# Rounding the attention input's high part on ScalarE instead of GpSimd, in a fused attention and routed-FFN kernel

## The chip, the cores and the metric

The kernel runs on one core of one Trainium2 chip. The metric is the device time of one execution in microseconds, the median of three runs. Everything is one program: a layer-norm with modulation, an attention whose probabilities are formed per head, a second layer-norm, and a feed-forward block that is applied to the best 512 tokens of each batch.

## The reference, cut to what matters

```python
sa, ca, ga, sb, cb, gb = mod[:, 0], ..., mod[:, 5]        # from silu(c) @ wmod
h = _layernorm(x) * (1 + ca) + sa                         # x: 8 x 1024 x 512, float32
q, k, v = h @ Wq + bq, h @ Wk + bk, h @ Wv + bv           # each reshaped to (b, 16 heads, 32, t)
attn = softmax(einsum('bhdt,bhds->bhts', k, v) * temperature)
x = x + ga * einsum('bhdt,bhts->bhds', q, attn)
h = _layernorm(x) * (1 + cb) + sb
# router scores, best 512 of 1024 tokens, gelu FFN 512 -> 2048 -> 512, scattered back
x = x + gb * FFN(h)
```

The change concerns the first `h` alone: the modulated input of the projections.

## The kernel before, in words

The attention runs over 32 groups of 256 rows (8 batches of GB = 4 groups). A group holds four heads, whose scores are 32 units of 128 x 1024, taken as 16 pairs. PSUM has three slots for units (`SLOTS = 3`), one bank `pj` for projections and one `acc` for the output. Each engine has its own program with the order of its work written out by hand, and semaphores alone tie them together:

- TensorE (`body` from L756): for each pair p it makes the scores of unit (p, 0), the products of pair p - 4 with the queries, the scores of unit (p, 1), and a piece of the next group's key, value or query projection (L657, L669). Scores wait until ScalarE has freed the slot of three units earlier.
- VectorE (`body`, L1250): the negated row maximum of each unit (L1142), and between these the division of the queries by the row sums (`q_over_sums`, L1189 and L1194, once per two pairs), gating (L1171), statistics (L1176, L1062), the router's dot product (L1162). In the first group alone it also clamps the gates in four instructions (`clamp_gates`, L1151 to L1157) behind pairs 4 and 5.
- ScalarE (`body`, L963): the exponential of each unit (L916), which waits for its maximum, and evacuations of the projections: a key or value piece (L887) between the two exponentials of pairs 2, 5, 8 and 11, queries at 13 and 15. In the first group it also moves the late modulation out of `acc` before pair 3's exponentials (L972).
- GpSimd (`body`, L1589): elementwise work in eight portions. A portion begins behind a division on VectorE (`behind_qn(b, g, j)`, which waits for the division that VectorE issues at pair 2j).
- SyncE's queue (`body`, L541) issues loads, stores, the replication of keys and values (L488), and the DMA transposes.

The input of group n is prepared two groups ahead. GpSimd normalises it into `xhat` and multiplies by the scale in its last portion (`begin_x`, L1453 and L1498). In portion 0 of the group after, it adds the shift (`plus_shift`, L1503), then rounds to the 16-bit high part `x16[:, 0]` (`high_x`, L1510). In portion 1 it makes the low part (`low_x`, L1515). SyncE waits for `s_hi` and issues four transposes of the high part, waits for `s_ht` and issues four of the low part (`transpose_x`, L480), and then goes on to wait for the residual and to load the next x (`load_x`, L441). In the first group it stores the clamped gates before all this (`store_modulation`, L509), behind `s_modv`, which the last clamp raises. The rounding occurs 30 times, in all groups but the last two.

Of the kernel before, what the change touches and what calls it, by code (L numbers as in the profile page):

```python
# [17 lines left out]
GB = T // TG  # L18
# [11 lines left out]
ALU = mybir.AluOpType  # L30
ACT = mybir.ActivationFunctionType
# [100 lines left out]
def block_phases(nc, x, w_qkv, b_qkv, temperature, w_router, w_ffn, c, w_mod, out, h_rows, mod_rows, first_rows, sel_rows, score_rows, r):  # L132
# [16 lines left out]
    with ExitStack() as ctx:  # L149
# [6 lines left out]
        def sem(name):  # L156
            return ctx.enter_context(nc.semaphore(name))
# [24 lines left out]
        xhat = room3[:, 0, 0:2, :]  # L182
# [9 lines left out]
        x16 = room2[:, S_LEN + 2 * KV_LEN:S_LEN + 3 * KV_LEN].rearrange("p (a s n) -> p a s n", a=2, s=SUBS)  # L192
# [129 lines left out]
        s_xm = sem("s_xm")  # L322
        s_xt = sem("s_xt")
# [8 lines left out]
        s_hi = sem("s_hi")  # L332
# [41 lines left out]
        def ring_at(p, h2):  # L374

            return 2 * p + h2
# [5 lines left out]
        def unit_no(b, g, u):  # L382

            return b * (GB * UNITS) + (g * UNITS + u + 1)

        def pair_no(b, g, p):

            return b * (GB * PAIRS) + (g * PAIRS + p + 1)

        def slot(b, g, v):  # L390

            return sc[:, ((b * GB + g) * RING + v) % SLOTS, :]

        def prepared(n):


            return 16 * 4 * SUBS * (n - 1)
# [235 lines left out]
        def stk_count(b, g):  # L633

            return b * (128 * GB // 2) + 128 * (g // 2 + 1)
# [237 lines left out]
        def _(act):  # L873
# [8 lines left out]
            def evac_kv(g, kk, count, free, src=pj[:]):  # L882

                act.wait_ge(kv_pe, count)
                if free is not None:
                    act.wait_ge(kv_split, free)
                nc.scalar.activation(kv32[kk % 2][:], src, ACT.Identity,  # L887
                                     scale=tempw_col[:, g:g + 1] if kk < 2 else 1.0 / WS).then_inc(kv_evac, 1)

            def evac_t(src, count, parts=False):  # L890

                act.wait_ge(t_pe, count)
                for cc in range(CC):
                    a = nc.scalar.activation(hT32[:, cc, :].rearrange("q (t s e) -> q s t e", t=2, s=SUBS),
                                             src[:, cc * 2 * P:(cc + 1) * 2 * P].rearrange("q (s t e) -> q s t e", t=2, s=SUBS),
                                             ACT.Identity, bias=mod_now[:, CC + cc:CC + cc + 1], scale=mod_now[:, cc:cc + 1])
                    if parts:
                        a.then_inc(t_part, 1)
                return a
# [10 lines left out]
            def exp_unit(b, g, p, h2):  # L910

                u = 2 * p + h2
                act.wait_ge(max_done, unit_no(b, g, u))
                if h2 == 0:
                    act.wait_ge(pv_done, pair_no(b, g, p))
                nc.scalar.activation(probs[:, u % PROBS, :], slot(b, g, ring_at(p, h2)), ACT.Exp,  # L916
                                     bias=nmax[:, u % PROBS:u % PROBS + 1],
                                     accum_out=rsum[:, (u // 4) % 2, u % 4:u % 4 + 1]).then_inc(slot_free, 1)

            act.wait_ge(s_now, 1)  # L920
            evac_t(sc[:, 2, :], 1, parts=True)
            act.wait_ge(s_bk, 2 * 16)
# [35 lines left out]
            def kept_high(n, cc, src):  # L958

                act.wait_ge(ft_pe, nth(n, CC, cc + 1))  # L960
                nc.scalar.activation(fT16[n % 2][0][:, cc, :], src, ACT.Identity).then_inc(ft_hi, 1)

            def body(b, last):  # L963
                for g in range(GB):
                    n4 = b * (GB * 4) + 4 * (g + 1)
                    n2 = b * (GB * 2) + 2 * (g + 1)
                    end = last and g == GB - 1
                    for p in range(PAIRS):
                        if b == 0 and g == 0 and p == LAG - 1:
                            act.wait_ge(pv_done, LAG)  # L970
                            act.wait_ge(s_one, 2)
                            nc.scalar.activation(mod_b, late_ps, ACT.Identity, bias=one_row[:, 0:1]).then_inc(s_modc, 1)  # L972
                        exp_unit(b, g, p, 0)
                        if p < 12 and p % 3 == 2 and not end:
                            evac_kv((g + 1) % GB, p // 3, n4 + p // 3 + 1, n4 + p // 3 - 1)
                        if (p == 13 or p == 15) and not end:
                            evac_q((g + 1) % 2, (p - 13) // 2, n2 + (p - 13) // 2 + 1)
                        if last and g == 1 and p == 2:
                            act.wait_ge(s_dot, 2 * (NG - 3) + 1)
                            nc.scalar.activation(r.e_neg[:, 0:LAST * TB], scores[:, AHEAD:AHEAD + LAST * TB], ACT.Exp, scale=-1.0).then_inc(s_exps, 1)  # L980
                        if end and p == 3:
                            for k in range(2):
                                for s in range(SUBS):
                                    act.wait_ge(s_stk[k][1][s], stk_count(LAST, GB - 1))
                            high_part(0)
                        if end and p == 11:
                            high_part(1)
                        if end and p - 1 in KEPT_AT:
                            kept_high(0, KEPT_AT.index(p - 1), aux[0])
                        exp_unit(b, g, p, 1)  # L990

            for b in range(B - 1):
                body(b, False)
# [420 lines left out]
        def _(pool):  # L1414
# [9 lines left out]
            for j in range(P // DH):  # L1424
# [4 lines left out]
                last = nc.gpsimd.affine_select(out=part, in_=part, compare_op=ALU.is_gt, fill=0.0, base=2 * DH * h2 + t,  # L1429
                                               pattern=[[-1, 2], [-2 * DH, 2], [-2, DH]], channel_multiplier=2)  # L1430
# [72 lines left out]
                nc.gpsimd.tensor_tensor(xhat, xhat, mod_x[:, 0:1, :].broadcast_to([P, SUBS, D]), ALU.add).then_inc(s_xm, 1)  # L1503
                pool.wait_ge(s_xm, 2 * (n - 1))

            def high_x(n):

                if n > 2:
                    pool.wait_ge(s_xt, prepared(n - 1))
                nc.gpsimd.tensor_scalar(x16[:, 0], xhat, 1.0, 1.0, ALU.mult, ALU.mult).then_inc(s_hi, 1)  # L1510

            def low_x(n):

                pool.wait_ge(s_hi, n + 1)
                nc.gpsimd.tensor_tensor(x16[:, 1], xhat, x16[:, 0], ALU.subtract).then_inc(s_ht, 1)  # L1515

            def begin_x(n):
# [71 lines left out]
            def body(b, last):  # L1589
                for g in range(GB):  # L1590
                    n4 = b * (GB * 4) + 4 * (g + 1)
                    n = b * GB + g + 2
                    nxt = (g + 1) % GB
                    prep = not (last and g >= GB - 2)
                    end = last and g == GB - 1

                    if b == 0 and g == 1:
                        pool.wait_ge(s_modst, 4 * 16)
                    behind_qn(b, g, 0)
                    if prep:  # L1600
                        plus_shift(n)
                        high_x(n)
                    if last and g == GB - 2:
                        store_kept(nc, r, sel_rows, range(2, 4))
                    if end:
                        gather_h(0, h_rows[0:T])
                    behind_qn(b, g, 1)
                    if prep:
                        low_x(n)
                    if not end:  # L1610
                        split_kv(nxt, 0, n4 + 1, n4 + 1 - 3)
                    if last and g == GB - 2:
                        store_kept(nc, r, sel_rows, range(4, 6))
                    behind_qn(b, g, 2)
                    residual(b, g)
                    if last and g == GB - 2:
                        store_kept(nc, r, sel_rows, range(6, TB))
                    if end:
                        break
                    behind_qn(b, g, 3)  # L1620
                    split_kv(nxt, 1, n4 + 2, n4 + 2 - 3)
                    normed_before(b, g)
                    behind_qn(b, g, 4)
                    h_times(b, g)
                    split_kv(nxt, 2, n4 + 3, n4 + 3 - 3)
                    behind_qn(b, g, 5)
                    h_plus(b, g)
                    split_kv(nxt, 3, n4 + 4, n4 + 4 - 3)
                    behind_qn(b, g, 6)
                    base_times(b, g)  # L1630
                    base_plus(b, g)
                    behind_qn(b, g, 7)
                    if n + 1 < NG:
                        begin_x(n + 1)
                    if last and g == GB - 3:
                        wait_alone(r.s_slot, 1)
                        store_kept(nc, r, sel_rows, range(0, 2))
# [76 lines left out]
```

## Time and profile before

| | |
|---|---|
| median of 3 runs | 2283.25 us (2282.88 to 2284.57) |
| the profiled execution's own time | 2283.22 us |
| its span, first to last instruction | 2281.5 us |
| TensorE busy | 2212.2 us (97%) |
| VectorE busy | 1890.5 us (83%) |
| ScalarE busy | 1431.7 us (63%) |
| GpSimd busy | 1398.7 us (61%) |
| mean granted TensorE clock | 0.993 of full speed |

The span is 1.7 us shorter than the execution's own time; that rest lies around the instructions. Busy shares are averages over two stages: the attention (to about 1,600 us), where VectorE is at nine tenths or more in every slice, and the feed-forward stage behind it, where VectorE falls to three to seven tenths.

### The profile page before, as it was taken

To read this page: it belongs to the slowest core of one execution; us is meant where nothing else is said; L and a number is where in the kernel's file an instruction comes from. 1 tells how busy PE (TensorE), PEld (TensorE's weight loads), DVE (VectorE), ACT (ScalarE), POOL (GpSimd) and SP (SyncE) were. 2 spreads that over 40 slices of the span, in tenths; PEclk is the share of its full clock that TensorE was granted. 3 is DMA by queue.
4 is the path that set the end of the run, shared out by engine and by line. 5 is a ranking of instruction groups with operands and counts; after the bars stand their busy time and mean duration, and the time that the engine had idled before them with its cause. 6 is when DMAs were issued, how large, how long until landed. Compare 5 with 4: busy or idle time off the path is not lost.

```text
span 2281.5 us, 35224 instructions
## 1 busy us (share of the span) xinstructions
PE 2212.2 (97%) x12410; PEld 840.0 (37%) x12410; DVE 1890.5 (83%) x2887; ACT 1431.7 (63%) x2478; POOL 1398.7 (61%) x1174
## 2 busy tenths in 40 slices
PE   6899999999999999999999999997899999999998
PEld 2233333333333333333333333331344444444443
DVE  6899999999999999999999999999873664563533
ACT  3688887888888888888888888888221111111110
POOL 6677887777888778887788877871642212302300
PEclk9999999999999999999999999999999999999999
DMA  7343344343335434444433533443432122112210
GB/s 255 79 104 88 92 108 96 95 103 95 91 90 122 84 93 114 85 101 100 98 89 89 127 82 91 97 84 94 139 88 70 41 66 70 61 47 70 68 31 19
DMA packets 218864, 206.06 MB, mean 90 GB/s; under 512 B 139256, under 2 KB 139288, under 8 KB 218176
## 3 DMA queue, kind: packets, MB, share of 16 engines
q1 hardware_dynamic: 208176, 174.12, 32.4%
q0 software_dynamic: 9728, 25.23, 3.5%
q10 hardware_dynamic: 784, 4.47, 0.5%
q8 instruction: 97, 1.59, 0.3%
q14 instruction: 79, 0.65, 0.1%
HBM read 71.37 MB, written 43.19 MB: 50 GB/s over the span
## 4 chain that ended last, share of the span: by engine, by line
PE 54%; DVE 32%; POOL 4%; issue 3%; SPq 3%; ACT 3%; DMA 1%; POOLq 0%; DVEq 0%; ACTq 0%
DVE nmax L1142 22%; PE sc L848 14%; PE sc L835 14%; PE sc L645 9%; PE acc L694 9%; PE pj L669 6%; POOL x L1530 3%; PE pj L657 3%; ACT probs L916 2%; DVE qn L1194 2%; DVE stats L1176 2%; DVE dot_out L1162 2%; SPq L480 1%; SPq L488 1%; DVE x L1171 1%
## 5 line engine op out<-in xcount | busy, mean ns | idle before, releaser
L916 ACT ACTIVATE probs<-sc,nmax 128x1024 f32<-128x1024 f32 x1024 | 1139.3, 1116 | 238.7 <-DVE nmax L1142 228.7
L1142 DVE TENSOR_REDUCE nmax<-sc 128x1 f32<-128x1024 f32 x1024 | 1206.1, 1212 | 28.3 <-PE sc L645 25.6
L694 PE MATMUL acc<-probs,qn 128*32 128x512 f32 x4096 | 546.6, 606 | 5.0 <-DVE x L1171 2.8
L1018 ACT ACTIVATE probs<-sc,b_col 128x512 f32<-128x512 f32 x128 | 87.9, 687 | 532.6 <-PE sc L835 519.1
L657 PE MATMUL pj<-room 128*128 128x512 f16 x1500 | 387.5, 381 | 2.7 <-POOL room L1483 2.7
L848 PE MATMUL sc<-room,probs 128*128 128x512 f16 x1536 | 355.5, 382 | 7.0 <-DVE probs L1362 4.1
L645 PE MATMUL sc<-room 128*128 128x512 f16 x1024 | 309.1, 384 | 23.1 <-ACT probs L916 13.7
L645 PE MATMUL sc<-stacks 128*128 128x512 f16 x1024 | 308.3, 383 | 11.7 <-ACT probs L916 10.2
L1360 DVE CAST probs<-probs 128x512 f16<-128x512 f32 x128 | 60.4, 472 | 292.1 <-ACT probs L1018 291.9
L848 PEld LDWEIGHTS sc<-room,probs 128*128 128x128 f16 x1536 | 150.8, 98 | 191.3 <-DVE probs L1362 5.0
L657 PEld LDWEIGHTS pj<-room 128*128 128x128 f16 x1500 | 144.2, 98 | 187.7 <-ACT room L887 12.2
L916 ACT ACTIVATION_READ_ACCUMULATOR probs<-sc,nmax 128x1 f32 x1024 | 202.8, 198 | 0.0
L669 PE MATMUL pj<-room 128*128 128x256 f16 x1512 | 185.6, 273 | 0.7 <-DVE room L1127 0.4
L645 PEld LDWEIGHTS sc<-room 128*128 128x128 f16 x1024 | 76.7, 98 | 294.1 <-ACT probs L916 196.0
L645 PEld LDWEIGHTS sc<-stacks 128*128 128x128 f16 x1024 | 75.9, 97 | 283.8 <-ACT probs L916 195.7
L835 PE MATMUL sc<-stacks,room 128*128 128x512 f16 x768 | 176.2, 379 | 0.0
L669 PEld LDWEIGHTS pj<-room 128*128 128x128 f16 x1512 | 147.0, 98 | 46.8 <-ACT qT L906 4.8
L694 PEld LDWEIGHTS acc<-probs,qn 128*32 128x32 f32 x4096 | 81.1, 108 | 224.0 <-issue 213.1
L1539 POOL TENSOR_TENSOR hbuf<-hbuf,rows 128x1024 f32<-128x1024 f32 x66 | 156.0, 2364 | 12.2 <-DVE qn L1194 8.9
L835 PE MATMUL sc<-qT,room 128*128 128x512 f16 x512 | 162.4, 379 | 0.0
L1472 POOL TENSOR_TENSOR room<-room 128x512 f16<-128x512 f32 x125 | 146.3, 1170 | 10.4
L1468 POOL TENSOR_TENSOR room<-room,k_bias 128x512 f32<-128x512 f32 x63 | 82.2, 1305 | 114.1 <-DVE qn L1194 109.1
(168 smaller groups left out, 2238.6 us busy)
## 6 DMA issues: line engine op xcount, KB each, us to landing
stacks<-room SPq DMA_DIRECT2D x512, 64.0 KB, 2.0
room<-room SPq DMA_DIRECT2D x508, 64.0 KB, 2.0
h_rows<-hbuf SPq DMA_DIRECT2D x132, 128.0 KB, 2.3
out<-base SPq DMA_DIRECT2D x132, 128.0 KB, 2.4
room<-in_L_attn_x SPq DMA_DIRECT2D x96, 128.0 KB, 2.6
rows<-mod_rows SPq DMA_DIRECT2D x32, 256.0 KB, 4.2
room<-in_L_ffn_W SPq DMA_DIRECT2D x8, 1024.0 KB, 5.3
probs<-in_L_wmod ACTq DMA_DIRECT2D x4, 1024.0 KB, 12.0
```

The costliest lines, as they stand in the source:

```text
L645: mm = nc.tensor.matmul(slot(b, g, v)[:, half * D:(half + 1) * D], stacks[g % 2][:, 0, hq, i * P:(i + 1) * P], stacks[g % 2][:, 1, hq, hal ...
L657: mm = nc.tensor.matmul(dst, hT16[par][:, a, cc, p * P:(p + 1) * P], w[:, z, cc, :], start=(t == 0), stop=(t == len(terms) - 1))
L669: mm = nc.tensor.matmul(dst[:, ci * 2 * P:(ci + 1) * 2 * P], wq16[:, z, cc, co * P:(co + 1) * P], hT16[par][:, a, cc, :], start=(t == 0), ...
L694: mm = nc.tensor.matmul(acc[at:at + DH, :], qn[:, (p // 2) % 2, p % 2, h2, :], probs[:, (2 * p + h2) % PROBS, half * D:(half + 1) * D], st ...
L835: mm = nc.tensor.matmul(ff[f % 2], w1_16[:, z, cc, f * P:(f + 1) * P], fT16[n % 2][a][:, cc, :], start=(t == 0), stop=(t == len(terms) - 1))
L848: mm = nc.tensor.matmul(ff2[kt], g16[:, nth(n, FC, f) % 3, a, kt * P:(kt + 1) * P], w2_16[:, z, f, :], start=(f == 0 and t == 0), stop=(f ...
L916: nc.scalar.activation(probs[:, u % PROBS, :], slot(b, g, ring_at(p, h2)), ACT.Exp, bias=nmax[:, u % PROBS:u % PROBS + 1], accum_out=rsum[ ...
L1018: nc.scalar.activation(g32[:, f % 2, :], ff[f % 2], ACT.Gelu_apprx_tanh, bias=b1_col[:, f:f + 1], scale=1.0 / WS).then_inc(gelu_done, 1)
L1142: nc.vector.tensor_reduce(nmax[:, u % PROBS:u % PROBS + 1], slot(b, g, ring_at(p, h2)), AX.X, ALU.max, negate=True).then_inc(max_done, 1)
L1468: nc.gpsimd.tensor_tensor(kv32[kk % 2][:], kv32[kk % 2][:], row, ALU.add).then_inc(kv_bias, 1)
L1472: nc.gpsimd.tensor_tensor(dst[:, 1], kv32[kk % 2][:], dst[:, 0], ALU.subtract).then_inc(kv_split, 1)
L1539: nc.gpsimd.tensor_tensor(dst, a, rows[:, row:row + 1, :].broadcast_to([P, SUBS, D]), op).then_inc(s_hm, 1)
```

## The change

ScalarE gets a function `high_x(n)`, called behind the second exponential of pair 1 in each of the 30 groups, and GpSimd loses its own. ScalarE's waits for the shift (`s_xm`), for the previous rounding (`s_hi`) and for the transposes that still read `x16` (`s_xt`). GpSimd's `low_x` now waits for ScalarE's rounding and for the same transposes.

```diff
@@ ScalarE
+            def high_x(n):
+                act.wait_ge(s_xm, 2 * (n - 1))
+                act.wait_ge(s_hi, n)
+                if n > 2:
+                    act.wait_ge(s_xt, prepared(n - 1))
+                nc.scalar.activation(x16[:, 0], xhat, ACT.Identity).then_inc(s_hi, 1)
...
                         exp_unit(b, g, p, 1)
+                        if p == 1 and not (last and g >= GB - 2):
+                            high_x(b * GB + g + 2)
@@ GpSimd
-            def high_x(n):
-
-                if n > 2:
-                    pool.wait_ge(s_xt, prepared(n - 1))
-                nc.gpsimd.tensor_scalar(x16[:, 0], xhat, 1.0, 1.0, ALU.mult, ALU.mult).then_inc(s_hi, 1)
...
             def low_x(n):
 
                 pool.wait_ge(s_hi, n + 1)
+                if n > 2:
+                    pool.wait_ge(s_xt, prepared(n - 1))
                 nc.gpsimd.tensor_tensor(x16[:, 1], xhat, x16[:, 0], ALU.subtract).then_inc(s_ht, 1)
...
                         plus_shift(n)
-                        high_x(n)
```

## Rows read from the trace of the kernel before

**Rows 1.** The page, part 4: the chain that ended last, shares by line.

```profile
DVE nmax L1142 22%; PE sc L848 14%; PE sc L835 14%; PE sc L645 9%; PE acc L694 9%; PE pj L669 6%; POOL x L1530 3%; PE pj L657 3%; ACT probs L916 2%; DVE qn L1194 2%; DVE stats L1176 2%; DVE dot_out L1162 2%; SPq L480 1%; SPq L488 1%; DVE x L1171 1%
```

**Rows 2.** Windows, one group: stretch, length, busy of PE, PEld, DVE, ACT, POOL, clock, DMA.

```profile
737.62:785.40 47.78, 47.54 (x293) 16.55 (x290) 46.66 (x65) 40.64 (x73) 38.21 (x32) 1.00 0.47 94
```

**Rows 3.** Timeline, GpSimd and VectorE, same group: start, length, instruction, idle before.

```profile
737.62 2.35 POOL L1503 TENSOR_TENSOR room<-room,f_lo 128x1024 f32<-128x1024 f32 x1 [0.32 <-DVE qn L1194]
740.06 1.36 POOL L1510 TENSOR_SCALAR room<-room 128x1024 f16<-128x1024 f32 x1
743.46 2.13 POOL L1515 TENSOR_TENSOR room<-room 128x1024 f16<-128x1024 f32 x1 [2.03 <-DVE qn L1194]
...
739.64 0.88 DVE L1162 SCALAR_TENSOR_TENSOR dot_out<-hbuf,router_row 128x512 bf16<-128x512 f32 x1
```

**Rows 4.** Timeline, ScalarE from the end of pair 1 to pair 3.

```profile
740.77 0.19 ACT L916 ACTIVATION_READ_ACCUMULATOR probs<-sc,nmax 128x1 f32 x1
741.70 1.11 ACT L916 ACTIVATE probs<-sc,nmax 128x1024 f32<-128x1024 f32 x1 [0.74 <-DVE nmax L1142]
742.80 0.68 ACT L887 ACTIVATE room<-pj,tempw_col 128x512 f32<-128x512 f32 x1
743.37 1.11 ACT L916 ACTIVATE probs<-sc,nmax 128x1024 f32<-128x1024 f32 x1
...
746.17 1.11 ACT L916 ACTIVATE probs<-sc,nmax 128x1024 f32<-128x1024 f32 x1 [0.50 <-DVE nmax L1142]
```

**Rows 5.** Groups by form, ScalarE rounding float32 to float16: busy us, mean ns.

```profile
L956 ACT ACTIVATE room<-room 128x2048 f16<-128x2048 f32 x8 | 15.3, 1907 | 13.7 <-DMA room<-in_L_ffn_W 13.7
```

**Rows 6.** Timelines of weight loads, matmuls and VectorE about pairs 3 and 4.

```profile
743.53 0.72 PEld L657 LDWEIGHTS pj<-room 128*128 128x128 f16 x4
...
746.16 0.60 PE L645 MATMUL sc<-room 128*128 128x512 f16 x2
...
744.92 3.47 DVE L1142 TENSOR_REDUCE nmax<-sc 128x1 f32<-128x1024 f32 x3
```

**Rows 7.** Timeline, GpSimd in the first group.

```profile
58.30 2.36 POOL L1503 TENSOR_TENSOR room<-room,f_lo 128x1024 f32<-128x1024 f32 x1 [0.21 <-DVE qn L1194]
...
67.66 2.35 POOL L1530 TENSOR_TENSOR x<-x,xt 128x1024 f32<-128x1024 f32 x1
```

**Rows 8.** Timeline, ScalarE in the first group.

```profile
56.18 1.11 ACT L916 ACTIVATE probs<-sc,nmax 128x1024 f32<-128x1024 f32 x1 [0.85 <-DVE nmax L1142]
...
58.94 0.69 ACT L972 ACTIVATE base<-acc,one_row 128x512 f32<-128x512 f32 x1
```

**Rows 9.** Timeline, VectorE in the first group.

```profile
59.67 0.69 DVE L1171 TENSOR_TENSOR x<-acc,rows 128x512 f32<-128x512 f32 x1 [0.29 <-ACT base L972]
...
63.67 0.63 DVE L1151 TENSOR_SCALAR hbuf<-base 64x512 f32<-64x512 f32 x1
64.23 1.75 DVE L1152 SCALAR_TENSOR_TENSOR hbuf<-base 64x512 f32<-64x512 f32 x1
...
66.10 0.50 DVE L1194 TENSOR_TENSOR qn<-qT,rinv 128x128 f32<-128x128 f32 x1
...
68.79 1.51 DVE L1155 TENSOR_SCALAR hbuf<-hbuf 64x512 f32<-64x512 f32 x1
```

**Rows 10.** Timelines of SyncE's queue and of VectorE, later in the first group.

```profile
71.04 1.31 SPq L509 DMA_DIRECT2D mod_rows<-base  x4
...
73.99 10.66 SPq L480 DMA_TRANSPOSE room<-room  x8
...
89.08 0.69 DVE L1062 BATCH_NORM_STATS2 stats<-xt 128x6 f32<-128x512 f32 x1 [6.63 <-DMA xt<-in_L_attn_x]
```

**Rows 11.** Windows in the first group, columns as in rows 2.

```profile
85.00:92.00 7.00, 0.95 (x8) 0.04 (x7) 2.92 (x4) 1.07 (x2) 1.60 (x2) 0.91 0.54 142
92.00:98.00 6.00, 5.81 (x18) 1.45 (x19) 4.49 (x7) 4.39 (x10) 4.36 (x4) 0.54 0.40 91
```

**Rows 12.** Source line L1162, all instances: duration ns, minimum/median/maximum.

```profile
L1162 DVE SCALAR_TENSOR_TENSOR dot_out<-hbuf,router_row x67: 679/852/1162, 54.0 to 1674.6; 128x512 bf16<-128x512 f32 x67
```

More of the change, by code:

```diff
@@ L1504, in plus_shift, with low_x @@
                 pool.wait_ge(s_xm, 2 * (n - 1))
-            def high_x(n):
+            def low_x(n):
+                pool.wait_ge(s_hi, n + 1)
                 if n > 2:
                     pool.wait_ge(s_xt, prepared(n - 1))
-                nc.gpsimd.tensor_scalar(x16[:, 0], xhat, 1.0, 1.0, ALU.mult, ALU.mult).then_inc(s_hi, 1)
-            def low_x(n):
-                pool.wait_ge(s_hi, n + 1)
                 nc.gpsimd.tensor_tensor(x16[:, 1], xhat, x16[:, 0], ALU.subtract).then_inc(s_ht, 1)
```

## The prediction

> **What bounds the kernel now.** I read the page's chain first. VectorE's row maximum holds 22% of it, far more than any other line of the attention [rows 1]. The windows then show how near the bound each engine is inside one group: of 47.78 us VectorE is busy 46.66 and ScalarE 40.64 [rows 2]. The reader is to see that VectorE has about 1.1 us to spare in a group, ScalarE 7.1 us, and TensorE (47.54 us, with modelled ends) little. GpSimd, the engine that is relieved, is busy 38.21 us and bounds nothing in this stretch. So what the change is worth is read from whether VectorE's order of work moves. I then went through the timelines at the place of the edit, first in an ordinary group, then in the first group, which stands differently.
>
> **Ordinary groups (29 of the 30).** Removed from GpSimd: one rounding of 1.36 us, at 740.06. Its next instruction, the low part, does not start when the rounding ends (741.42) but at 743.46, behind VectorE's division [rows 3]. So the removal starts nothing earlier on GpSimd; its idle time before the low part grows from 2.03 to about 3.4 us. Price: nothing, hidden by the wait for the division.
>
> Added to ScalarE: one rounding of 128 x 1024. The trace has none of this shape. From below, half of the 128 x 2048 rounding is 0.95 us [rows 5]; from above, the 128 x 1024 exponential is 1.11 us [rows 4]. I take 1.05, as the fixed part of an instruction is not halved. What it waits for is there: the shift ends at 737.62 + 2.35 = 739.97 [rows 3], and the read-out of pair 1's second exponential ends at 740.77 + 0.19 = 740.96 [rows 4]. Neighbouring instructions on ScalarE overlap by about a tenth (the evacuation ends at 743.48, the next exponential starts at 743.37 [rows 4]). So the rounding runs from 740.87 to 741.92, and the next exponential can start at 741.81 in place of 741.70. The 0.74 us for which ScalarE waited there [rows 4] takes nearly all of it; 0.11 us is left. In other groups this idle time differs by a tenth or so, and I allow 0.1 to 0.25.
>
> Who waits for that lag? Queued behind the rounding are the exponential of unit (2, 0), the evacuation of a key piece, and the next exponentials. The evacuation ends at 743.48 and TensorE loads weights for the next piece at 743.53 [rows 6], so TensorE can come up to 0.1 us late there. It passes that on to the scores of unit (4, 1), which now end at 746.16 + 0.60 = 746.76. The reduction that reads them is the third of the three from 744.92, each about 1.13 us apart, so it starts at 747.18 [rows 6]: 0.42 us to spare. ScalarE has 0.50 us idle before the exponential at 746.17 [rows 4], and its lag ends there. VectorE sees nothing: price 0 per group. If that cover were gone, it would be 0.11 to 0.25 us times 29, which is 3.2 to 7.3 us. From below, no gain either, except by rival four.
>
> SyncE is moved too: the four transposes of the high part start about 0.5 us later (741.92 for 741.42). Eight take 10.66 us in the queue [rows 10]. What stands behind them, the residual's wait and the loads of x, moves by the same half microsecond; it is needed at pair 9, seven pairs of 3 us later. GpSimd's added wait on the old transposes is one that it already had. Price 0.
>
> **The first group.** Here GpSimd is late. Its shift starts at 58.30 and ends at 60.66 [rows 7], while ScalarE starts unit (2, 0) at 56.18 after 0.85 us of idling [rows 8]. With the edit ScalarE stands at the rounding until 60.66, rounds for 1.05 us, and starts unit (2, 0) at about 61.67. That is 5.5 us later. Everything queued behind it moves by as much, among it L972, which takes the late modulation out of `acc` at 58.94 [rows 8] and would do so at 64.4. VectorE's gating at 59.67 waited for exactly this, by 0.29 us [rows 9], and moves to 65.2. From there VectorE runs without a gap through three maxima, two clamps, the division, two maxima and the other clamps. At its end SyncE starts storing the gates at 71.04 [rows 10].
>
> Some of the 5.5 us comes back, because VectorE's instructions in this stretch are now slowed by GpSimd, which will have become idle by then (it waits for the division of pair 4). L1152 takes 1.75 us [rows 9]. Its twin L1157 fits between the end of L1155 (68.79 + 1.51 = 70.30 [rows 9]) and 71.04 [rows 10], so it takes 0.7; 1.05 come back. L1151 (0.63) and the division (0.50) [rows 9] are slowed in the same way by an estimated half: 0.5 together. L1155 then starts 3.95 us later, at 72.74. It now ends 0.29 us after the residual on GpSimd does (67.66 + 2.35 = 70.01 [rows 7]), so it waited for that. The residual starts behind the division, which will be at 66.10 + 5.5 - 1.35 = 70.25 to 70.55, plus 0.15 for the signal: 70.7 to 73.05. L1155 then ends at 73.3 in place of 70.3. **3.0 us are left** of 5.5. The ends of this term are 2.5 (a little more comes back) and 5.5 (nothing does).
>
> These 3.0 us are on the path. The queue runs from 71.04 without a real pause: gates, eight transposes from 73.99, then the load of x, and VectorE stands idle 6.63 us for that load until 89.08 [rows 10]. All later groups hang on VectorE.
>
> **Sum.** 29 x 0 + 3.0 on the profiled execution's own 2283.22 us (span 2281.5 and 1.7 around it) is 2286.2. That execution lies 0.03 under the median, so I forecast 2286.3 us. A measurement of this kernel can tell about 0.2%, that is 4.6 us, from no change; the forecast is slower, by less than that.
>
> **Rivals.**
>
> *One: the stall arrives whole, and TensorE's clock falls.* Scores of unit (3, 1) need the slot that the late exponential frees, so TensorE stands still some 5 us before 62.9. After the quiet stretch from 85 to 92 (0.95 us busy in 7) the granted clock was 0.54 from 92 to 98, which is the 1.2 GHz level [rows 11]. At that level the products and scores ahead of the pair 4 maximum (about 1.6 us at full clock) cost about 1 us more than VectorE's work hides. With no give-back: 5.5 + 1.0 = 6.5, so 2289.8 us. For it: the stand-still is real. Against it: the pause here is shorter, and the slowed rows are plain. By the Trainium skill ("TensorE: Matmul & The Clock Gate", section "What's actually happening") an idle TensorE goes back to 1.2 GHz; the trace agrees for the longer pause (0.54), and no row shows one of 5 us.
>
> *Two: the lag of ordinary groups passes.* 3.0 + 3.2 to 7.3 gives 2289.5 to 2293.6 us. It decides from a lag of 0.42 us at unit (4, 1) in the group shown. The 0.1 us margins of other groups speak for it, the 0.50 us idle against.
>
> *Three, the other side: the first group's wait swallows the stall.* VectorE idles 6.63 us at 82.45 to 89.08 anyway, more than 5.5. If the load of x did not hang on the clamps, the delay would vanish there: 2283.3 us, no change. It decides as long as the stall stays under 6.63 us and the load keeps its time. Against it: the queue is in order, and the store of the gates starts with the last clamp's end [rows 10].
>
> *Four: VectorE is freed of contention.* The router's dot product takes 0.88 us beside GpSimd [rows 3] and 0.68 at its fastest [rows 12]. If the rounding were what slows it, 0.2 x 29 = 5.8 us would come back: 2283.3 + 3.0 - 5.8 = 2280.5 us. Against it: the dot product starts at 739.64, the shift ends at 739.97, and 739.97 + 0.55 is where it ends; the rounding starts only at 740.06 [rows 3], when the dot product is already under way. The Trainium skill says ("GPSIMD Engine Reference", section "1. Specifications") that the two engines share their SBUF interfaces, VectorE instructions with two SBUF inputs among those that contend. By that rule the removal should bring the 5.8 us; the trace agrees that there is contention (0.88 against 0.68) but puts it on the shift, which stays.
>
> **How the numbers follow.** Chances: forecast 0.55, rival one 0.17, two 0.10, three 0.12, four 0.06. The forecast's own range is 2285.7 to 2288.0. Leaving out rival four, the lower edge of three and the upper half of two, the range for 8 in 10 is 2283.0 to 2290.5 us. Slower by over 0.2% (over 2287.8): rivals one and two and a small part of the forecast, 0.31. Faster by over 0.2%: most of rival four, 0.05. Within: 0.64.
>
> **What the changed profile would show.** ScalarE: 30 roundings of 1.05 us, one of them in the first group behind some 5.3 us of idling for the shift, the others behind none. The exponential behind it 0.1 to 0.25 us late in ordinary groups, the length of a group unchanged (47.8 us for the one shown). GpSimd idle 3.4 us before the low part. VectorE's gating in the first group near 65.2, L1152 near 0.7 us, the gates stored near 74.0, the statistics of x near 92.1. I would be wrong if ordinary groups change their length, if ScalarE waits for the shift in them, or if the store of the gates is late by less than 2.5 or more than 5.5 us.

## The result, and the profile after

| | before | changed |
|---|---|---|
| median of 9 runs | 2283.25 us (2281.28 to 2285.91) | 2290.69 us (2289.64 to 2291.60) |
| span of the profiled execution | 2281.5 us | 2288.8 us |

The ratio is 1.003, with a 95% interval of 1.002 to 1.004: slower by 7.4 us, where 3.0 were forecast. The measured median lies 0.2 us beyond the upper end of the stated range (2290.5).

The ordinary groups first. The timelines of ScalarE, GpSimd and VectorE in the changed kernel, in the same group that [rows 3, 4, 6] show of before:

```profile
747.06 0.19 ACT L916 ACTIVATION_READ_ACCUMULATOR probs<-sc,nmax 128x1 f32 x1
747.15 1.04 ACT L926 ACTIVATE room<-room 128x1024 f16<-128x1024 f32 x1
748.10 1.10 ACT L916 ACTIVATE probs<-sc,nmax 128x1024 f32<-128x1024 f32 x1
...
752.49 1.11 ACT L916 ACTIVATE probs<-sc,nmax 128x1024 f32<-128x1024 f32 x1 [0.43 <-DVE nmax L1152]
```

```profile
743.92 2.37 POOL L1513 TENSOR_TENSOR room<-room,f_lo 128x1024 f32<-128x1024 f32 x1 [0.32 <-DVE qn L1204]
749.82 2.14 POOL L1521 TENSOR_TENSOR room<-room 128x1024 f16<-128x1024 f32 x1 [3.54 <-DVE qn L1204]
...
754.09 1.16 POOL L1482 TENSOR_TENSOR room<-room 128x512 f16<-128x512 f32 x1
```

```profile
749.30 0.29 DVE L1204 TENSOR_TENSOR qn<-qT,rinv 128x128 f32<-128x128 f32 x1
...
754.84 0.57 DVE L1204 TENSOR_TENSOR qn<-qT,rinv 128x128 f32<-128x128 f32 x1
```

The rounding takes 1.04 us and waits for nothing; the exponential behind it starts about 0.1 us after it could have, and ScalarE idles again (0.43 us) two units on. But GpSimd's low part starts at 749.82, which is 0.23 us behind the end of VectorE's division (749.30 + 0.29). In the kernel before it started at 743.46 [rows 3] against a division that ended at 743.27 (the first row below), 0.19 us. In the unrounded times of all 29 ordinary groups this distance is 0.18 us before; in the changed kernel it is 0.23 to 0.24, but for one group with 0.54. GpSimd's three instructions of the key split then all end later. VectorE's division of pair 4 ends 0.16 us behind the last of them in both kernels (755.41 against 755.25, and 749.04 against 748.88), and takes 0.57 us where it took 0.52. The rows of before:

```profile
742.98 0.29 DVE L1194 TENSOR_TENSOR qn<-qT,rinv 128x128 f32<-128x128 f32 x1
...
748.52 0.52 DVE L1194 TENSOR_TENSOR qn<-qT,rinv 128x128 f32<-128x128 f32 x1
```

```profile
747.72 1.16 POOL L1472 TENSOR_TENSOR room<-room 128x512 f16<-128x512 f32 x1
```

The first group, against [rows 7 to 10]. ScalarE and VectorE of the changed kernel:

```profile
59.62 1.06 ACT L926 ACTIVATE room<-room 128x1024 f16<-128x1024 f32 x1 [5.13 <-POOL room L1513]
60.59 1.10 ACT L916 ACTIVATE probs<-sc,nmax 128x1024 f32<-128x1024 f32 x1
...
63.33 0.69 ACT L980 ACTIVATE base<-acc,one_row 128x512 f32<-128x512 f32 x1
```

```profile
64.06 0.69 DVE L1181 TENSOR_TENSOR x<-acc,rows 128x512 f32<-128x512 f32 x1 [5.73 <-ACT base L980]
...
67.86 1.23 DVE L1152 TENSOR_REDUCE nmax<-sc 128x1 f32<-128x1024 f32 x1 [0.85 <-PE sc L645]
69.00 0.41 DVE L1161 TENSOR_SCALAR hbuf<-base 64x512 f32<-64x512 f32 x1
69.34 0.68 DVE L1162 SCALAR_TENSOR_TENSOR hbuf<-base 64x512 f32<-64x512 f32 x1
...
70.14 0.29 DVE L1204 TENSOR_TENSOR qn<-qT,rinv 128x128 f32<-128x128 f32 x1
...
72.61 0.64 DVE L1165 TENSOR_SCALAR hbuf<-hbuf 64x512 f32<-64x512 f32 x1
...
92.12 0.69 DVE L1072 BATCH_NORM_STATS2 stats<-xt 128x6 f32<-128x512 f32 x1 [6.70 <-DMA xt<-in_L_attn_x]
```

ScalarE stands 5.13 us for the shift, VectorE 5.73 us for the late modulation. (The attention started 2.0 us earlier in this execution, at 45.3 us for 47.3, and lost about 1 us of that at once, in two waits for the scores of pair 1. So single times of this group can be compared with those of before only to about 1 us.) The four slowed instructions are fast now: 0.41, 0.68, 0.29 and 0.64 us for 0.63, 1.75, 0.50 and 1.51 [rows 9]. New is the 0.85 us wait for scores at 67.86. A window of the changed kernel shows TensorE's clock there (the number before the last two), and its timeline the idle time ahead of it:

```profile
63.00:66.00 3.00, 3.00 (x10) 0.81 (x12) 1.94 (x3) 2.21 (x6) 2.72 (x3) 0.50 0.03 5
```

```profile
61.83 1.03 PE L645 MATMUL sc<-room 128*128 128x512 f16 x2 [4.72 <-ACT probs L916]
```

After 4.72 us of standing still TensorE had the 1.2 GHz level (granted 0.50). Its clock fell to that level behind the stall in all three profiles of the changed kernel, but VectorE paid for it differently: 0.85, 1.11 and 0 us.

A third place had not been looked at. The group that begins at about 350 us is 51.3 us long before and 54.4 after. VectorE waits there for the next x; the row of before, then that of the changed kernel:

```profile
378.72 0.69 DVE L1062 BATCH_NORM_STATS2 stats<-room 128x6 f32<-128x512 f32 x1 [2.92 <-DMA room<-in_L_attn_x]
```

```profile
383.40 0.69 DVE L1072 BATCH_NORM_STATS2 stats<-room 128x6 f32<-128x512 f32 x1 [5.25 <-DMA room<-in_L_attn_x]
```

SyncE's queue in that group: it stores the router's scores, waits until they have landed, loads them (L523), and only then issues the transposes and the load of x. Before, then changed:

```profile
353.00 0.44 SPq L519 DMA_DIRECT2D score_rows<-scores  x1
363.22 0.34 SPq L523 DMA_DIRECT2D srow<-score_rows  x1
363.67 10.84 SPq L480 DMA_TRANSPOSE room<-room  x8
```

```profile
355.63 0.45 SPq L519 DMA_DIRECT2D score_rows<-scores  x1
367.50 0.34 SPq L523 DMA_DIRECT2D srow<-score_rows  x1
367.95 11.11 SPq L480 DMA_TRANSPOSE room<-room  x8
```

From store to load of the scores it is 10.2 us before and 11.9 after. These are the first profiles; two more of each kernel follow below, and they lie closer together.

### The profile page after: what moved, and what is told of

Same layout as the page of the kernel before. It is cut to its first block, busy times and chain, and to the rows that moved or that the text cites. A ratio compares the mean times of both kernels' runs of the same rounds, so it can differ in the third digit from the quotient of the medians.

```text
span 2288.8 us, 35254 instructions
## 1 busy us (share of the span) xinstructions
PE 2218.1 (97%) x12410; PEld 842.3 (37%) x12410; DVE 1891.8 (83%) x2887; ACT 1456.5 (64%) x2508; POOL 1353.7 (59%) x1144
## 4 chain that ended last, share of the span: by engine, by line
PE 55%; DVE 32%; POOL 4%; issue 3%; ACT 3%; SPq 2%; DMA 1%; POOLq 0%; DVEq 0%; ACTq 0%
DVE nmax L1152 22%; PE sc L848 14%; PE sc L835 14%; PE sc L645 9%; PE acc L694 9%; PE pj L669 6%; POOL x L1536 3%; PE pj L657 3%; ACT probs L916 2%; DVE qn L1204 2%; DVE stats L1186 2%; DVE dot_out L1172 2%; SPq L480 1%; DVE x L1181 1%; SPq L488 1%
## 5 line engine op out<-in xcount | busy, mean ns | idle before, releaser
L1545 POOL TENSOR_TENSOR hbuf<-hbuf,rows 128x1024 f32<-128x1024 f32 x66 | 155.9, 2362 | 14.6 <-DVE qn L1204 11.3
```

Of the source, the lines that this page charges most:

```text
L1545: nc.gpsimd.tensor_tensor(dst, a, rows[:, row:row + 1, :].broadcast_to([P, SUBS, D]), op).then_inc(s_hm, 1)
```

## The experiments

All were timed in five rounds against the kernel before, except the two third profiles. The median of the unaltered kernel before differed by 1.0 us between these sessions (2282.50 to 2283.49), so gains are taken against the kernel before of the same session. The table gives lengths from the first maximum of one group to the first of the next, from VectorE's timelines of each profile: group 0, groups 1 to 5 together, group 6 (the one at 350 us), groups 7 to 30 together.

| kernel | median us (before beside it) | ratio, 95% | 0 | 1-5 | 6 | 7-30 |
|---|---|---|---|---|---|---|
| before, 3 profiles | 2283.25 | | 62.9, 63.0, 63.1 | 237.1, 237.1, 237.1 | 51.3, 52.2, 51.7 | 1144.9, 1145.1, 1144.8 |
| changed, 3 profiles | 2290.69 (2283.25) | 1.003 (1.002-1.004) | 66.7, 68.1, 66.2 | 237.6, 237.7, 237.7 | 54.4, 53.4, 52.9 | 1146.9, 1147.2, 1147.3 |
| first_on_gpsimd | 2285.18 (2283.49) | 1.0009 (1.0000-1.0018) | 62.9 | 237.4 | 53.0 | 1146.2 |
| first_alone | 2286.05 (2283.49) | 1.0011 (1.0002-1.0021) | 66.0 | 237.0 | 52.9 | 1144.4 |
| one_wait | 2286.19 (2283.49) | 1.0011 (1.0002-1.0020) | 66.4 | 237.1 | 53.0 | 1145.6 |
| scores_later_before | 2278.23 (2282.50) | 0.9980 (0.9971-0.9989) | 62.1 | 237.0 | 47.4 | 1144.7 |
| scores_later_after | 2283.44 (2282.50) | 1.0002 (0.9993-1.0011) | 66.0 | 237.6 | 47.4 | 1147.0 |
| combined | 2278.46 (2282.50) | 0.9979 (0.9970-0.9988) | 63.5 | 237.3 | 47.4 | 1144.1 |
| x_first_after | 2285.43 (2282.83) | 1.0009 (0.9999-1.0018) | 60.7 | 239.5 | 52.5 | 1146.8 |
| x_first_best | 2275.57 (2282.83) | 0.9968 (0.9956-0.9980) | 58.6 | 239.1 | 47.4 | 1145.2 |

**The changed kernel again, twice.** No edit.

> The changed kernel unaltered, for a second profile on the chip of its siblings. Theory A (the stall of the first group is the main loss, the ordinary groups lose 0.05 us each behind GpSimd's second wait): the first group about 3.8 us longer than the 62.9 of before, ordinary groups 0.04 to 0.05 longer, 5 to 8 us over the kernel before. On the group that begins at about 350 us, which grew from 51.3 to 54.4 us: if that is chance of one execution, this profile has it near 51.3 again; if it belongs to the change, near 54.4.

> The changed kernel unaltered, a third profile, for the same group (54.4 and 53.4 us in the first two). If its length belongs to the change: 53 to 54.5; if it is chance: anywhere from 51 to 54.4. The first group 66 to 68 us, ordinary groups as in the first two.

Timed again, the changed kernel had 2289.82 us against 2283.49, ratio 1.0026 (1.0015 to 1.0037); the third profile's execution took 2289.72. Mean lengths of three profiles, changed less before: 4.0 us in group 0, 0.6 in groups 1 to 5, 1.8 in group 6, 2.2 in groups 7 to 30, together 8.6. The attention started 0.6 us earlier on average and the rest of the kernel was 0.5 shorter, which leaves the 7.5 us between the spans. Group 1 begins 3.4 us later on average (113.2 us for 109.9), and the gates are stored at 74.00, 74.23 and 73.94 us for 71.04, 71.21 and 70.58, 3.1 us later. So the first group costs 3.1 to 4.0 us, depending on where it is measured from. Group 6 varies (52.9 to 54.4) but stayed above the kernel before's.

**The kernel before again, twice.** No edit.

> The kernel before unaltered, for a second profile. Equal time within 0.1%. If the group at about 350 us (51.3 us long, where ScalarE and VectorE wait for the next x) varies from one execution to another, it shows here as a length away from 51.3; the start of the first group (47.3 us) shows how much the opening varies.

> The kernel before unaltered, a third profile, for the length of the group at 350 us (51.3 and 52.2 us in the first two). If its length belongs to the kernel: 51 to 52.5; if it is chance: anywhere from 51 to 54.4.

The second gave 2282.87 us against 2282.50, ratio 1.0000 (0.9991 to 1.0009). Group 6 took 52.2 and 51.7 us. The opening, up to the first maximum, varied by 0.7 us (46.6 to 47.3).

**The first group's rounding back on GpSimd (first_on_gpsimd).**

```diff
-                        if p == 1 and not (last and g >= GB - 2):
+                        if p == 1 and (b or g) and not (last and g >= GB - 2):
                             high_x(b * GB + g + 2)
@@ GpSimd
                         plus_shift(n)
+                        if n == 2:
+                            high_first()      # tensor_scalar into x16[:, 0], as before
```

> The changed kernel, but the first group's rounding stays on GpSimd and ScalarE has the other 29. Theory A: the first group is back at 62.9 us, VectorE's gating there no longer waits 5 us, the ordinary groups keep their 0.045 us each (1.3 us); 1 to 4.5 us over the kernel before, so 3 to 6 under the changed one. Rival (the lag of ScalarE in the ordinary groups is the loss): nearly the same time as the changed kernel, 6 to 7.5 us over the kernel before.

1.7 us over the kernel before and 4.6 under the changed one. Group 0 is back at 62.9 us, and VectorE's gating waits 0.28 us, as before:

```profile
58.96 0.69 DVE L1181 TENSOR_TENSOR x<-acc,rows 128x512 f32<-128x512 f32 x1 [0.28 <-ACT base L980]
```

The ordinary groups keep an excess of 1.6 us (0.3 and 1.3), which is 29 times 0.05, and the low part is 0.23 to 0.24 us behind the division in every one of them. The rival that puts the whole loss on ScalarE's lag is out.

**The first group's rounding alone on ScalarE (first_alone).** The other 29 stay on GpSimd.

```diff
+            def high_first():
+                act.wait_ge(s_xm, 2)
+                act.wait_ge(s_hi, 2)
+                nc.scalar.activation(x16[:, 0], xhat, ACT.Identity).then_inc(s_hi, 1)
...
                         exp_unit(b, g, p, 1)
+                        if b == 0 and g == 0 and p == 1:
+                            high_first()
@@ GpSimd
-                        high_x(n)
+                        if n > 2:
+                            high_x(n)
```

> The kernel before, but the first group's rounding alone is on ScalarE behind pair 1; the other 29 stay on GpSimd. Theory A: the first group 3 to 4 us longer, ordinary groups as before to 0.02 us; 3 to 6 us over the kernel before (the upper end if the group at 350 us grows with it). Rival (ordinary groups are the loss): within 1.5 us of the kernel before.

2.6 us over the kernel before, 0.4 short of the expected 3 to 6; the interval of the ratio, 0.5 to 4.8 us, holds part of that. Group 0 is 3.0 us longer than the mean of before, the ordinary groups are not. So the stall costs about 3 us by itself, and one rounding suffices for it.

**One wait less on GpSimd (one_wait).**

```diff
             def low_x(n):
                 pool.wait_ge(s_hi, n + 1)
-                if n > 2:
-                    pool.wait_ge(s_xt, prepared(n - 1))
                 nc.gpsimd.tensor_tensor(x16[:, 1], xhat, x16[:, 0], ALU.subtract).then_inc(s_ht, 1)
```

> The changed kernel without GpSimd's second wait in low_x (the one for the old transposes, which ScalarE's rounding has already waited for). Theory A: GpSimd starts the low part 0.18 us behind VectorE's division instead of 0.23 to 0.24, the division of pair 4 takes 0.52 instead of 0.57, each ordinary group is 0.045 us shorter, together 1.3 us: 5 to 6.5 us over the kernel before. Rival (the 0.05 us comes from ScalarE's lag): nothing changes, the pair 4 division stays at 0.57.

3.6 us under the changed kernel timed beside it. That is more than the 1.3 expected, but the interval of either kernel is 2 to 2.5 us to each side, and 0.6 us each lie in groups 0 and 6, which vary by more than that between executions. Its timelines in the group of the rows above:

```profile
748.05 2.14 POOL L1519 TENSOR_TENSOR room<-room 128x1024 f16<-128x1024 f32 x1 [3.48 <-DVE qn L1204]
```

```profile
747.59 0.29 DVE L1204 TENSOR_TENSOR qn<-qT,rinv 128x128 f32<-128x128 f32 x1
...
753.12 0.51 DVE L1204 TENSOR_TENSOR qn<-qT,rinv 128x128 f32<-128x128 f32 x1
```

The low part is 0.17 us behind the division again (748.05 against 747.88), in all 29 groups, and the division of pair 4 takes 0.51. ScalarE's rounding is where it was, so the 0.05 us per group is the wait's and not ScalarE's lag. Groups 1 to 5 are at the length of before, groups 7 to 30 lose 1.5 of their 2.2 us. The sum is more than 29 x 0.05 because three groups of the changed kernel lose 0.3 us more, in all three of its profiles: groups 5 and 10 at the division of pair 4 and group 12 further on. This part is not the wait's: first_on_gpsimd has the wait in all 29 groups and none of these losses, while one_wait still loses 0.3 in group 10 (and 0.6 in group 26), and combined (below), without the wait too, in groups 5 and 12. Why they occur was not found.

**The scores' wait moved behind the load of x**, in the kernel before (scores_later_before) and in the changed one (scores_later_after).

```diff
-                    if b * GB + g == RANK_FROM:
-                        sp.wait_ge(s_sc, 16 * 2)
-                        load_scores(0)
...
                         load_x((g + 3) % 4, ahead[g])
+                    if b * GB + g == RANK_FROM:
+                        sp.wait_ge(s_sc, 16 * 2)
+                        load_scores(0)
```

> The kernel before, with SyncE's wait for the stored router scores and their load moved behind the transposes and the load of x in the one group that has it. Theory A (the group at 350 us is long because the queue stands 10 us for the scores' store and x comes late): this group falls from 51.3 to 47.9 us, VectorE's 2.9 us wait for x is gone, 3.3 us faster than the kernel before. Rival (that group is long for its added counting on VectorE): 0.5 us or less gained.

> The changed kernel with the same edit of SyncE's order. Theory A: the group at 350 us falls from 54.4 to 47.9 us, 6 us less than the changed kernel if its 3.1 us growth is systematic, 3.3 if it was chance; 0.5 to 4.5 us over the kernel before. Rival: as the changed kernel, 7 us over.

Group 6 falls to 47.4 us in both. The kernel before gains 4.3 us. The changed kernel was 6.3 us over the kernel before (after_again) and is 0.9 over it with this edit, a gain of 5.4; in the profiles group 6 falls by 4.3 and 6.2 us. The queue of the changed kernel with this edit starts the transposes 1.7 us after the scores' store instead of 12.3:

```profile
356.66 0.45 SPq L519 DMA_DIRECT2D score_rows<-scores  x1
358.40 11.47 SPq L480 DMA_TRANSPOSE room<-room  x8
369.91 1.99 SPq L441 DMA_DIRECT2D room<-in_L_attn_x  x4
371.94 0.42 SPq L523 DMA_DIRECT2D srow<-score_rows  x1
```

So the changed kernel's excess in group 6 needs this wait. The six profiles show where it arises. On average x lands 1.4 us later after the start of the group: the store of the scores is issued 0.4 us later, it is 11.3 us from it to their load in place of 10.5, and the transposes take 0.3 us more. The remaining 0.4 goes with TensorE's clock. It fell to a granted 0.50 behind the wait for x in all three profiles of the changed kernel (TensorE stood 4.0 to 4.9 us there) and in one of the three of before (3.5 us, against 2.5 and 3.0 where it stayed at 1.00), and VectorE then waited 0.7 to 1.5 us for scores. Why x is late by those 1.4 us is not settled: the kernels with only a part of the change, and x_first_after, have 52.5 to 53.0 us too, while the three profiles of before have 51.3 to 52.2.

**All three cures together (combined)**: first rounding on GpSimd, one wait less, scores later (the diffs above).

> Changed kernel, first group's rounding on GpSimd, no second wait in low_x, scores later. Theory A: every known loss is gone, so the time is that of the kernel before with the scores later, 3 us under the kernel before, and no better than that, since ordinary groups gain nothing from the freed 1.4 us of GpSimd. Rival (the freed time is worth something once the losses are gone): clearly under the kernel before with the scores later.

2278.46 us, against 2278.23 for the kernel before with the scores later alone. With its side effects gone, the move of 29 roundings from GpSimd to ScalarE costs nothing and gains nothing that can be measured: the intervals leave room for some 3 us either way, and in the profiles groups 1 to 5 and 7 to 30 are together 0.3 us shorter than in scores_later_before. A large gain, the rival's, is out.

**The first group's x loaded first**, in the changed kernel (x_first_after), and in the kernel before with the scores later (x_first_best).

```diff
                         if b == 0:
+                            sp.wait_ge(x2_done, 1)
+                            load_x(3, ahead[0])
                             store_modulation()
...
-                    if not (last and g >= GB - 3):
+                    if not (last and g >= GB - 3) and (b or g):
                         load_x((g + 3) % 4, ahead[g])
```

> The changed kernel, with the first group's load of x issued before the gates are stored and the transposes, once the residual that reads the old x is done. Theory A (the stall reaches the end through SyncE's queue: the last clamp, the gates' store, eight transposes, the load, VectorE's 6.6 us idle at pair 9): that idle time disappears and the first group falls by 5 to 6 us from 66 to 68, 4 to 6 us less than the changed kernel. Rival (the stall goes through VectorE alone, and the queue is only beside it): less than 2 us gained.

> The kernel before with the scores later and the first group's load of x first. Theory A: the first group falls from 62 to 63 us to 57 or 58, the group at 350 us stays at 47.4; 8 to 10 us under the kernel before. Rival: as with the scores later alone, 4 us under.

On the changed kernel group 0 falls by 6.3 us from the mean of three, to 60.7, and VectorE's 6.7 us wait is gone, but groups 1 to 5 give back 1.8. The kernel is 2.6 us over the kernel before, where the unaltered changed one was 6.3 over it, a gain of 3.7 us (4 to 6 expected). The theory holds: the stall had reached the end through the queue. The second kernel, at 2275.57 us, is 7.3 us under the kernel before (ratio 0.9968, 0.9956 to 0.9980) and beats both; the 8 to 10 us expected were too much, for the same 2 us are given back in groups 1 to 5. The traces show what holds them back. At the end of group 0 VectorE waits for the first scores of group 1, in x_first_best:

```profile
104.57 1.23 DVE L1144 TENSOR_REDUCE nmax<-sc 128x1 f32<-128x1024 f32 x1 [3.19 <-PE sc L647]
```

TensorE starts these scores at 103.94 us. They read the replicated keys and values, and the last of the transfers that they wait for, the 24th of 32 that the queue issues behind the transposes, landed at 103.86 (in x_first_after 106.03 and 105.94). TensorE had stood for 3.6 and 3.4 us, its granted clock fell to 0.50, and group 1 is 2 us longer. So the queue is the limit again, one transfer further on.

## Why the prediction was right or wrong, point by point

**Right: what bounds, and no gain.** The freed 1.36 us became idle time before the low part (3.54 us, 3.4 expected), and combined shows that it is worth nothing. Rival four is out: the router's dot product is no shorter (median 0.85 us in both kernels).

**Right: ScalarE's part of the ordinary groups.** The rounding's 1.04 us (1.05 taken), no wait for the shift, a lag of about 0.1 that ends within two units. Rival two, that this lag passes to VectorE, is out by one_wait and combined.

**Wrong: "GpSimd's added wait on the old transposes is one that it already had. Price 0."** The step looked at whether the semaphore would be satisfied, not at where the wait stands. Before, it was passed in portion 0, ahead of the rounding, with nothing late behind it. Now it stands between VectorE's division and the low part, at the head of a chain of four GpSimd instructions whose end holds up VectorE's next division. It costs 0.05 us in each group, 1.5 us in all; first_on_gpsimd shows this sum alone (1.6) and one_wait takes it away. In the profiles the ordinary groups cost 2.8 us (0.6 + 2.2), where 0 was forecast; 1.0 of it are the three groups that lose 0.3 us more, whose cause is open. "I would be wrong if ordinary groups change their length" came true, by a wait that the prediction had put at nothing.

**First group: right, and its size within what the executions can tell.** The stall (5.5 us; ScalarE's wait was 5.13 and the gating's 5.73), the four give-backs and the way through SyncE's queue came as worked out. The give-back at the gates' store was expected as 2.5 us: from the rows it is 0.2 + 1.1 + 0.2 + 0.9 = 2.4. The 3.0 us forecast measured 3.1 to 4.0 in the means, single profiles of group 0 lie 3.2 to 5.1 over the mean of before, and first_alone 3.0. The half of rival one that concerns TensorE came too, in part: the clock fell after 4.72 us of standing still, in every profile with the stall, and cost VectorE 0.85 and 1.11 us in two of the three profiles. The forecast had put this at nothing. The third profile had the low clock and no wait, and its group 0 grew by 3.2 us. That the gates' store and the statistics of x came within 0.1 us of the times predicted (74.00 and 92.12, for 74.0 and 92.1) is in part luck, as this execution had started 2.0 us earlier.

**Right in kind: the load of x.** Rival three did not come: VectorE's idle time before the load stayed (6.70 us for 6.63) and moved as a whole; x_first_after took it away.

**Not foreseen: group 6.** The prediction looked for one kind of exception, the first group, and missed the second one that the timeline shows, a group of 51.3 us among groups of 47.4. It brings 1.8 us in the profiles, and 1.1 by the difference of the two scores_later gains (5.4 - 4.3), which the noise of the medians does not tell from 1.8. Its place is shown, its cause is open.

So of 7.4 us the first group holds 3 to 4, the ordinary groups 2 to 3 and group 6 one to two. (In the profiles the groups sum to 8.6, less a start that happened to be 0.6 us earlier and 0.5 behind the attention.)

**Close by luck.** The totals of rivals one (2289.8 us) and two (from 2289.5) lie within 1.2 us of the measured time, and they are why the stated range reached so far up. Neither came: rival one had no give-back, and rival two wanted ScalarE's lag to pass to VectorE. What filled the gap is the wait on GpSimd and group 6, which are in no sum of the prediction, and a share of the clock.

## What to carry to other kernels

A wait that is always satisfied has a price, if it is issued between a late signal and work whose end holds up another engine: here 0.05 us on GpSimd, 29 times. Put waits ahead of the late one, or drop those that the signal already implies. Before work is moved to an engine that never waits for its input in the steady state, look at every group that differs from the steady one; one group of 32 held about half of this loss, and a second such group, an in-order queue standing 10 us for a store to land, was worth 4.3 us by itself to the kernel before.

## What the runs showed of the hardware that was not expected

A VectorE instruction of 64 x 512 took 0.68 us alone and 1.75 us beside GpSimd's elementwise work; one that starts beside GpSimd's residual took 1.51 us and 0.64 beside its last part only. The four slowed instructions of the first group [rows 9] each ended 0.1 to 0.5 us after the end of the GpSimd instruction that was running when they were issued. Landing 1,024 scores of 4 bytes took 10.2 to 11.9 us from issue to the next instruction of the queue, in the ten profiles in which the queue waited for it. Two satisfied waits on GpSimd in place of one moved the next instruction from 0.17 or 0.18 us behind VectorE's signal to 0.23 or 0.24.
